# Attention with a second score pass that has keys on partitions: first pass for row maxima only, sums of exponentials on GpSimd

## The reference

```
proj = x @ W_in.T + b_in                      # 16 heads, q, k and v of 64 columns each
q, k = rope(q), rope(k)
att  = softmax(causal_mask(q @ k.T / 8))      # 1024 x 1024 for each batch and head
y    = att @ v
x    = layernorm(x + y @ W_out.T + b_out)
x    = layernorm(x + moe(x))                  # 16 experts, top 3: not touched but for how x is read in
```

## Time and profile before

| | us |
|---|---|
| median of three runs | 2156.67 |
| the profiled execution, whole | 2156.06 |
| its span, first to last instruction | 2154.3 |
| attention phase (from the start to the last output add) | 1503.3 |
| PE busy | 1934.3 |
| DVE busy | 1437.1 |
| ACT busy | 970.1 |
| POOL busy | 648.0 |

### The profile page before, as it was taken

How to read it: one execution, slowest core, us unless ns; L and a number is a source line. 1 busy time by engine, 2 the same in 40 slices (tenths; PEclk the granted TensorE clock), 3 DMA queues, 4 the chain that set the end, 5 groups by cost and what they waited for, 6 DMA issues and landing times. The chain is left out here.

```text
span 2154.3 us, 41980 instructions
## 1 busy us (share of the span) xinstructions
PE 1934.3 (90%) x12431; PEld 1471.7 (68%) x12433; DVE 1437.1 (67%) x2985; ACT 970.1 (45%) x2299; POOL 648.0 (30%) x603
## 2 busy tenths in 40 slices
PE   4699998999999999899999989998568999999950
PEld 4577776776677677677667767765235999999950
DVE  4477776776777677677677767775597444444438
ACT  3355554555555455455555545554533222122225
POOL 2123222232222222223222322220223555555545
PEclk8799999999999999999999999999755999999985
DMA  9643344333353434433435333440900222222246
GB/s 324 196 104 93 79 97 129 90 89 80 77 123 86 119 79 95 106 77 89 119 78 122 87 80 79 103 105 8 366 21 18 71 71 71 69 69 71 71 151 199
DMA packets 103739, 223.91 MB, mean 104 GB/s; under 512 B 22065, under 2 KB 58097, under 8 KB 102657
## 3 DMA queue, kind: packets, MB, share of 16 engines
...
## 5 line engine op out<-in xcount | busy, mean ns | idle before, releaser
L671 DVE TENSOR_REDUCE negm<-s_ps 128x1 f32<-128x640 f32 (+7 forms) x512 | 383.6, 752 | 230.7 <-PE s_ps L456 209.1
L614 ACT ACTIVATE prob<-s_ps,negm 128x640 f32<-128x640 f32 (+7 forms) x512 | 378.9, 741 | 211.4 <-DVE negm L671 160.2
L538 PE MATMUL t_ps<-ident,prob 128*128 128x128 f32 x2304 | 356.3, 282 | 33.3 <-ACT pT L641 11.7
L389 POOL TENSOR_TENSOR roped<-rot 128x512 f32<-128x512 f32 x128 | 182.8, 1428 | 668.1 <-DVE rot L680 652.4
L641 ACT ACTIVATE pT<-t_ps 128x512 f32<-128x512 f32 (+1 forms) x416 | 214.2, 531 | 337.6 <-PE t_ps L538 240.2
L553 PE MATMUL y_ps<-pT,v_sb 128*64 128x256 f32 (+1 forms) x2560 | 356.8, 379 | 0.0
L538 PEld LDWEIGHTS t_ps<-ident,prob 128*128 128x128 f32 x2304 | 257.0, 142 | 129.6 <-issue 72.7
L452 PE MATMUL s_ps<-k,q 128*128 128x512 f32 (+3 forms) x768 | 315.4, 411 | 8.0 <-ACT v_sb L630 6.0
L393 POOL TENSOR_TENSOR lo<-roped,hi 128x512 fp32r<-128x512 f32 x128 | 165.0, 1289 | 414.6 <-ACT hi L622 414.6
L697 DVE TENSOR_SCALAR prob<-prob,rden 128x640 f32<-128x640 f32 (+7 forms) x512 | 282.8, 574 | 3.4
L454 PE MATMUL s_ps<-k,q 128*128 128x512 f32 (+3 forms) x768 | 263.6, 355 | 0.0
...
## 6 DMA issues: line engine op xcount, KB each, us to landing
q<-hi SPq DMA_DIRECT2D x256, 128.0 KB, 2.3
q<-lo SPq DMA_DIRECT2D x256, 128.0 KB, 2.3
...
k<-hi SPq DMA_DIRECT2D x128, 128.0 KB, 2.3
k<-lo SPq DMA_DIRECT2D x128, 128.0 KB, 2.3
...
```

What stands on the lines that cost most here:

```text
L389: nc.gpsimd.tensor_tensor(roped[:], rot[:, 0, :], rot[:, 1, :], ALU.subtract if half else ALU.add).then_inc(m["added"], 1)
L538: ins = nc.tensor.transpose(bank[:, o:o + P], prob[q % 2][:, h, ii, j * P:(j + 1) * P], ident[:])
L614: nc.scalar.activation(prob[q % 2][:, h, blk % 2, 0:w], scores(bank, banks)[:, 0:w], ACT.Exp, bias=negm[:, s, i:i + 1], scale=1.0, accum_o ...
L671: nc.vector.tensor_reduce(negm[:, s, i:i + 1], scores(*score_banks(f"S{i}"))[:, 0:w], AX_X, ALU.max, negate=True).then_inc(m["max_done"], 1)
```

## The change

The scores are computed twice.

- **A, first pass**: queries on partitions, only the product of q1 with k1, and only the row maximum is taken from it (M). There are 12 units for each head: blocks 0 to 3 whole, blocks 4 to 7 in two pieces, since each head has one bank of PSUM (`a_ps`). A unit waits for the maximum of the unit before it.
- **X, w, put_max**: PE transposes the negated maxima (X), ACT copies them to SBUF (w), SP sends them by DMA into row 64 of q2. Row 64 of the new operand k2 holds ones, so that the second product of B subtracts the maximum.
- **B, second pass**: keys on partitions, 12 units for each head (`key_unit`: a half of the queries and a block of keys), two products, the mask where the unit has the diagonal. ACT writes the exponentials to SBUF, where they stand as V needs them.
- **Gone**: the transposes U with their copies u, the scaling P, the accumulated row sums.
- **Sums**: POOL adds the exponentials of the key blocks (k for the first half of the queries, K for the second: 11 adds in a step, 256 to 1024 elements on each partition). PE sums over partitions with a matrix of ones (D), ACT copies the sum (d), DVE takes reciprocals of 128 x 128 (R, 8 in a step) and multiplies y by them (G).
- **V** takes units of up to 512 queries, 12 in a step.
- **Copies**: `stack_qk` still has 24 DMAs of the same size, 16 for q1 and k1, then 8 for q2 and k2. It now also waits until B of the step two before is complete. The copies of the maxima follow in SP's stream.
- **x1** holds two batches in SBUF during attention. SP stores each finished batch to DRAM, and the next phase loads all four.

The tables have new order. A stands one step ahead of B, F two ahead. PE's turn begins with the last A units of the step, and the first A of the next step (A0.0+) stands after B1.0 and A11.1; the last unit of the turn is B11.1.

```diff
+PE_ORDER = parse("""A9.1 B0.0 A10.0 B0.1 A10.1 A11.0 V8- V9- V10- V11- B1.0 A11.1 A0.0+ B1.1 B2.0 A0.1+ A1.0+ X1 B2.1 A1.1+ B3.0
+A2.0+ F0++ B3.1 B4.0 O0- A2.1+ B4.1 A3.0+ V0 D1- V1 V2 V3 A3.1+ A4.0+ B5.0 F1++ X0+ B5.1 A4.1+ A5.0+ B6 O1-
...
+POOL_ORDER = parse("""K10- k0 K11- k1 k2 k3 a0++ l0++ a1++ l1++ K5 a2++ K6 l2++ K7 a3++ K8 l3++ K9""")
+
+UNITS = 12
+P_PLACE = (1536, 2560, 3328, 3840, 0, 1024, 2048, 3072, 4096, 0, 768, 1280)
...
             def stack_qk(n, s):
 
 
+                wait_for(sp, b_fill[0], UNITS * (n - 1), n - 2)
+                wait_for(sp, b_fill[1], UNITS * (n - 1), n - 2)
                 sp.wait_ge(m["hi_done"], 4 * n + 4)
                 sp.wait_ge(m["lo_done"], 4 * n + 4)
                 for h in range(2):
...
+                                            (k1[s][h][pos:pos + 32], hi, k_in),
+                                            (k1[s][h][64 + pos:96 + pos], lo, k_in)):
                             sp.dma_start(dst.bitcast(F32), src[i:i + 32, f, :].bitcast(F32)).then_inc(qk_ld[s], 16)
+                for h in range(2):
+                    q_in, k_in = 32 * h, 64 + 32 * h
+                    for f in range(2):
+                        pos = 32 * f
+                        for dst, src, i in ((q2[s][h][pos:pos + 32], lo, q_in), (k2[s][h][pos:pos + 32], hi, k_in)):
+                            sp.dma_start(dst.bitcast(F32), src[i:i + 32, f, :].bitcast(F32)).then_inc(qk2_ld[s], 16)
+
+            def put_max(n, s, c):
+
+                sp.wait_ge(m_row[c], n + 1)
+                for h in range(2):
+                    sp.dma_start(q2[s][h][64:65, 512 * c:512 * c + 512].rearrange("a (i q) -> a i q", q=P).bitcast(F32),
+                                 mrow[c][4 * h:4 * h + 4, :].bitcast(F32)).then_inc(m_ld[c], 16)
 
...
+            def turn(it, place):
+
+                s = place % 2
+                if valid(it + 1):
+                    stack_qk(it + 1, 1 - s)
+                if valid(it):
+                    put_max(it, s, 1)
+                if valid(it + 1):
+                    put_max(it + 1, 1 - s, 0)
+                if valid(it + 2):
+                    n, last = it + 2, (place + 2) % PAIRS == PAIRS - 1
+                    more = last and valid(n + 1)
+                    if more:
+                        sp.wait_ge(m["p_fill"], 4 * n + 1)
+                        load_x((n + 1) // PAIRS, 0)
+                    sp.wait_ge(m["p_fill"], 4 * n + 2)
+                    sp.dma_start(flat(w_sb[s]), row(wsplit, (place + 4) % PAIRS)).then_inc(w_ld[s], 16)
...
+            def store_x(it, b):
+
+                sp.wait_ge(m["o_done"], 4 * it)
+                sp.dma_start(row(xacc, b).rearrange("p (t d) -> p t d", d=D),
+                             x1[:, b % 2 * TB:b % 2 * TB + TB, :] if isinstance(b, int) else
+                             x1[:, bass.ds(b % 2 * TB, TB), :]).then_inc(m["x_st"], 16)
+
...
+                    elif kind == "k":
+                        w = key_unit(q)[2]
+                        for h in range(2):
+                            pool.wait_ge(exp_done[h], UNITS * n + q + 1)
+                        sums = acc[:, 0, :, 512 - w:512]
+                        if q == 0:
+                            wait_for(pool, m["d_fill"], 2 * (n - 1) + 1, n - 1)
+                            ins = nc.gpsimd.tensor_tensor(acc[:, 0, :, 0:P], probs(0)[:, :, 0:P], ones[:, 0:1].rearrange("p (a c) -> p a c", a=1).broadcast_to([P, 2, P]), ALU.mult)
+                        elif q == 1:
+                            ins = nc.gpsimd.tensor_tensor(sums, probs(0)[:, :, P:512], probs(1), ALU.add)
+                        else:
+                            pool.wait_ge(m["sum_d"], D_SUMS * n + q)
+                            ins = nc.gpsimd.tensor_tensor(sums, sums, probs(q), ALU.add)
+                        ins.then_inc(m["sum_d"], 1)
+                    elif kind == "K":
+                        w = key_unit(q)[2]
+                        for h in range(2):
+                            pool.wait_ge(exp_done[h], UNITS * n + q + 1)
+                        if q == 5:
+                            wait_for(pool, m["d_fill"], 2 * n, n - 1)
+                            sums, old = acc[:, 1], probs(4)
+                        else:
+                            pool.wait_ge(m["sum_p"], P_SUMS * n + q - 5)
+                            sums = old = acc[:, 1, :, 512 - w:512]
+                        nc.gpsimd.tensor_tensor(sums, old, probs(q), ALU.add).then_inc(m["sum_p"], 1)
+
...
+            def query_scores(s, h, u):
+
+                blk, k0, w, diagonal = query_unit(u)
+                out = a_ps[:, h, 0:w]
+                ins = nc.tensor.matmul(out, q1[s][h][:, blk * P:(blk + 1) * P], k1[s][h][:, k0:k0 + w], start=True,
+                                       stop=not diagonal, skip_group_check=True)
+                if diagonal:
+                    ins = nc.tensor.matmul(out[:, w - P:w], identb[:], maskb[:], start=False, stop=True,
+                                           skip_group_check=True)
+                ins.then_inc(a_fill[h], 1)
+
+            def key_scores(s, h, k):
+
+                half, j, w = key_unit(k)
+                out, js, qs = b_ps[:, h, 0:w], slice(j * P, j * P + P), slice(512 * half + 512 - w, 512 * half + 512)
+                diagonal = j >= 4 * half
+                nc.tensor.matmul(out, k1[s][h][:, js], q1[s][h][:, qs], start=True, stop=False, skip_group_check=True)
+                ins = nc.tensor.matmul(out, k2[s][h][0:65, js], q2[s][h][0:65, qs], start=False, stop=not diagonal,
+                                       skip_group_check=True)
+                if diagonal:
+                    ins = nc.tensor.matmul(out[:, 0:P], maskb[:], identb[:], start=False, stop=True,
+                                           skip_group_check=True)
...
+                    if kind == "A":
+                        h = int(e[-1])
+                        if q == 0:
                             pe.wait_ge(qk_ld[s], 16 * QK_DMAS * (n // 2 + 1))
-                        score_fill(s, int(e[1:]))
+
+                        wait_for(pe, a_max[h], UNITS * n + q, n if q else n - 1)
+                        query_scores(s, h, q)
+                    elif kind == "B":
+                        h = int(e[-1])
+                        if q == 0:
+                            if isinstance(n, int) and n == 0:
+                                pe.wait_ge(m["ones_row"], 4)
+                            pe.wait_ge(qk2_ld[s], 16 * QK2_DMAS * (n // 2 + 1))
+                        if q in (0, 4):
+                            pe.wait_ge(m_ld[q // 4], 32 * (n + 1))
+
+                        wait_for(pe, exp_done[h], UNITS * n + q, n if q else n - 1)
+                        key_scores(s, h, q)
...
+                    elif kind == "D":
+                        if q == 0:
+                            pe.wait_ge(m["sum_d"], D_SUMS * (n + 1))
+                        else:
+                            pe.wait_ge(m["sum_p"], P_SUMS * (n + 1))
+                        for h in range(2):
+                            ins = nc.tensor.matmul(t_ps[64 * h:64 * h + 64, :], ones[:], acc[:, q, h, :],
+                                                   start=True, stop=True, skip_group_check=True)
+                        ins.then_inc(m["d_fill"], 1)
+                    elif kind == "X":
+                        if q == 0:
+                            for h in range(2):
+                                pe.wait_ge(a_max[h], UNITS * n + 4)
+                        else:
+                            pe.wait_ge(m["max_all"], n + 1)
+                        maxima = (max_a, max_c)[q][:, s].rearrange("p h i -> p (h i)")
+                        nc.tensor.transpose(t_ps[0:8, 0:P], maxima, ident[:]).then_inc(m["turned"], 1)
...
-                        w = (blk + 1) * P
-                        bank, banks = score_banks(f"S{i}")
-                        act.wait_ge(m["max_done"], S_PER * n + i + 1)
-                        if i % 4 == 0:
-
...
-                        nc.scalar.activation(prob[q % 2][:, h, blk % 2, 0:w], scores(bank, banks)[:, 0:w], ACT.Exp,
-                                             bias=negm[:, s, i:i + 1], scale=1.0,
-                                             accum_out=den[:, s, i:i + 1]).then_inc(m["exp_done"], 1)
+                        h, w = int(e[-1]), key_unit(q)[2]
+                        act.wait_ge(b_fill[h], UNITS * n + q + 1)
+                        if h == 0:
+
...
+                            elif q == 9:
+                                act.wait_ge(m["sum_p"], P_SUMS * n + 1)
+                        nc.scalar.activation(probs(q)[:, h, :], b_ps[:, h, 0:w], ACT.Exp).then_inc(exp_done[h], 1)
+                    elif kind == "w":
+                        act.wait_ge(m["turned"], 2 * n + q + 1)
+                        wait_for(act, m_ld[q], 32 * n, n - 1)
+                        nc.scalar.activation(mrow[q][:], t_ps[0:8, 0:P], ACT.Copy).then_inc(m_row[q], 1)
```

(27 more changed lines are left out.)

594 lines of the change are left out of this document (278 added, 316 removed).

## The result

The changed kernel takes 2364.38 us (median of 4 runs, 2360.77 to 2369.36); the kernel before takes 2156.92 us beside it (2151.82 to 2157.63). The ratio is 1.097, with a 95% interval of 1.094 to 1.100. Forecast were 2402 us (2310 to 2495). The profiled execution spans 2367.6 us, against 2154.3 before: +213.3.

The account below looks back on a forecast made before the run. PE's stream bounded the old kernel; in the new one a circle through the stack copies sets the turn. 2156.06 + 205 + 4 + 20 + 16 = 2401 us (2402 for the profiled execution), range 2310 to 2495.

Parts of the forecast that it names:

- The circle: Last B unit to stack copies to A0.0+: 12.1 us, leaving PE idle 6.1 us; turn at least 49.0 us.
- The issue's price: SP's queue: stack copies are issued one each 0.636 us, landing 2.3 us after issue.
- the circle doesn't bind: Rival on the stack copies: they come sooner, by an earlier b_fill or fewer bytes; 2208 us, chance 0.08.
- The second gate: Copies of the maxima ahead of B4.0: done 18.5 us into the turn, PE there at 18.4; costs nothing more.
- POOL's l3: POOL's last add, which the stack also waits for: comes before the last B unit, hidden by 3 us.
- PE's work in a turn: PE's units summed over a turn: from 42.5 us to 42.9 us, bounds 37.3 and 46.3.
- the transposes are not saved: On PE, the second pass over the scores (A, 7 us) takes the place of the transposes U (8.5 us).
- The clock: PE's clock falls after each turn's wait: 2.0 us lost a turn, bounds 0 and 2.8.
- the clock holds: Rival on PE's clock: no loss, so the turn is 49.0 us; 2344 us in all, chance 0.15.
- The turn: PE's turn with wait, clock and loop restarts: 51.5 us against 44.42, +205 us over 29 intervals.
- the loads of a batch: SP's store and load of a finished batch, 1 MB each, at three places: costed at nothing.
- Ends: Outside the 29 intervals: start +4, end of attention +20, x1's store and reload +16 us (8 to 25).

Follow-up runs that it names:

- Experiment 2: Changed kernel with B1.1, B2, X1, B3 and V0 to V3 moved ahead of A0.0+ in PE's order: 2239.09 us, ratio 1.038.
- experiment 10: Changed kernel with 24 stack copies of 64 partitions x 512 columns (128 KB), first column halves issued in the old step: 2065.80 us, ratio 0.958.
- experiment 5: Changed kernel with each stack copy cut into two of 512 columns (64 KB), A0.0+ waiting for 16 first halves: 2801.28 us, ratio 1.298.
- experiment 8: Changed kernel with each pair of stack copies merged into one of 64 partitions (256 KB), same place: 2379.53 us, ratio 1.105.
- experiment 11: The merged 128 KB copies of experiment 10, but all issued behind the old step's last B unit: 2307.87 us, ratio 1.072.
- experiment 4: Changed kernel with POOL's eleven adds cut to 32 columns of each head: 2364.91 us, ratio 1.099.
- experiments 1: Changed kernel with 24 unread products of 512 columns added on PE right ahead of A0.0+: 2307.63 us, ratio 1.070.

## Why the prediction was right

- **The circle** (last B unit, 16 issues, landing, A0.0+, rest of the turn, last B unit): recorded 12.1 us and 6.1 of idle time, measured 12.49 and 6.2 to 6.4 in the turns shown. Experiment 2 takes most of it away by order, experiment 10 all of it by earlier copies. Shown.
- **The issue's price** of 0.636 us: measured the same, and experiment 5 shows that fewer bytes don't lower it. That it is a price per copy holds up to 128 KB; experiment 8 shows the price by bytes above that, for which the prediction had no term and needed none. Of the rival "the circle doesn't bind", its "fewer bytes speed the issues" is refuted.
- **The second gate** at 18.5 against PE at 18.4: in the kernel after PE comes to B4.0 at 887.19, 22.1 us after the last B unit, since all from A0.0+ to F0 runs at the low clock (0.50 from 877.54 to 882.59) and F0 for the most part too (0.62). It comes some 3.6 us after the gate; experiment 11 shows the gate itself at 18.3.
- **POOL's l3** was to be hidden by 3 us. In the trace it ends at 913.62 and the mask of the last B unit starts at 915.12, so by 1.5, and experiment 4 shows that POOL doesn't matter. Its adds of 1024 elements take 2389 ns where the line through the two rows gave 2.7 us; by the figure for 2048 in the Trainium skill (GPSIMD Engine Reference, section on side-by-side cycle accounting) half would be an estimated 2.25, which is nearer. The sharing of SBUF access with VectorE shows in one instruction: G takes 1348 ns beside POOL's long adds and 982 beside the short ones of experiment 4. The Trainium skill (GPSIMD Engine Reference, section Key points) names contention with DVE instructions that have two SBUF inputs, and G is one. The reductions, which read PSUM, take 674 to 686 ns for 512 columns against 687 before. G stands twice in a turn, so this costs DVE 0.7 us of a turn in which it has 20 to spare.
- **PE's work in a turn** is the term that was mis-sized: recorded 42.9 us, measured 39.65 (experiments 1 and 10). Summed by line from one start to the next, the transposes were 8.3 (8.5) and A takes 6.8 (7). But the score products fell from 11.8 to 11.4 where I had 0.8 more, V fell by 1.9 instead of 1.2, mainly because the 0.15 us that I charged for each unit is paid once for a run of units (V8 to V11 with 1280 columns take 2.30 us from 867.75 to 870.05, which is 5 x 0.43 + 0.15), and O and F, for which I had no term, by 1.0 together. So my sentence that the transposes are not saved is wrong: the change takes 2.9 us a turn from PE, and the wait hides it.
- **The clock**: recorded 2.0 us a turn, with 2.8 as upper bound. PE's work is 42.54 and 43.65 us in the two turns shown against 39.65 at 1.00: 2.9 to 4.0. The rival "the clock holds" is refuted. The rule cited from the Trainium skill (TensorE: Matmul & The Clock Gate, section HAM oscillation) agrees with the trace: of the waits for copies ahead of A0.0+, all but one in the phase have a granted clock of 0.50 to 0.58 in the 3 us behind them. The one is 2.04 us long, at 1180.02, and the clock stays at 1.00.
- **The turn**: these two errors have opposite signs, 3.25 us too much work and 0.9 to 2.0 us too little for the clock, and it is partly luck that the turn came out this near. 39.65 + 6.3 + 2.9 to 4.0 is 48.9 to 50.0 us; what is left up to 50.28 belongs to turns with a longer leg: 14.4 to 14.6 us in those where the loop body starts again, for which 0.5 us a turn was recorded, and 15.4 us in one in which a load of 1 MB into xT (SP at 811.62) runs beside the stack's copies, so that PE waits 9.06 us at 828.45. There are three such waits, of 9.1 to 9.6 us, where the prediction costed the loads of a batch at nothing. The turn was recorded as 51.5, and 29 intervals gave +170 instead of +205. That is nearly all of the 38 us by which the forecast was too high.
- **Ends**: start +10.9 (4), tail +27.1 (20), the store and the load of x_now and what follows +5.5 (16). The sum is 43.5 instead of 40.
